# Query-key attention layer: three of four quads of value rows weighed by VectorE, one by POOL, and scans that start from PSUM

## What is computed

```python
q = (x @ Wq + bq).reshape(n, 8, 32); k = ...; v = ...
scores = einsum('ehd,ehd->eh', q[src], k[dst]) / sqrt(32)
m = segment_max(scores, dst)
e = exp(scores - m[dst])
z = segment_sum(e, dst)
p = e / maximum(z[dst], 1e-16)
out = segment_sum(v[src] * p[:, :, None], dst)
```

## Time and profile before

| what | value |
| --- | --- |
| median of three runs | 6924.0 us (6918.83 to 6942.32) |
| the profiled execution | 6916.7 us |
| its span | 6914.9 us |
| mean granted TensorE clock over the span | 0.808 |
| the changed stage in the span | about 3160 to 4556 us |

### The profile page before, as it was taken

One profiled execution on the slowest core, in us unless ns is written; L12 is line 12 of the kernel. 1 busy time (PEld: TensorE's weight loads), 2 busy tenths in 40 slices (PEclk: granted clock), 3 DMA queues, 4 the chain that ended last, 5 costly groups with the idle time before them and its releaser, 6 DMA issues. The chain is left out here.

```text
span 6914.9 us, 124558 instructions
## 1 busy us (share of the span) xinstructions
PE 4848.1 (70%) x21021; PEld 3523.0 (51%) x21022; DVE 5023.9 (73%) x11704; ACT 3845.9 (56%) x9024; POOL 4869.6 (70%) x4954
## 2 busy tenths in 40 slices
PE   6563277777647777775777777769999974777775
PEld 5452155555435555554555555546667653455553
DVE  6665377777757777787888888875555556777777
ACT  2341277677637676753444444426777763666664
POOL 0576677777477777757778878757777765777773
PEclk9655578788868888788989998979999985877777
DMA  5222255555335555525666666624444433555553
GB/s 166 66 70 53 80 135 137 135 137 135 92 92 136 136 135 137 134 77 147 187 178 187 181 187 179 184 72 130 129 130 130 130 102 103 136 135 135 135 134 91
DMA packets 596188, 894.68 MB, mean 129 GB/s; under 512 B 322611, under 2 KB 372960, under 8 KB 595700
## 3 DMA queue, kind: packets, MB, share of 16 engines
q0 software_dynamic: 245984, 649.30, 34.4%
q1 hardware_dynamic: 349700, 218.85, 11.9%
q10 hardware_dynamic: 416, 25.60, 1.1%
HBM read 859.36 MB, written 59.47 MB: 133 GB/s over the span
## 5 line engine op out<-in xcount | busy, mean ns | idle before, releaser
L1501 POOL DMA_INDIRECT at_ring<-tab_s,at_idx x808 | 776.0, 960 | 277.3 <-issue 204.7
L2391 POOL DMA_INDIRECT ae_ring<-tab_a,ae_idx x808 | 772.5, 956 | 256.0 <-issue 228.1
L1501 POOL DMA_INDIRECT at_ring_0a<-tab_s,at_idx_0a x808 | 767.5, 950 | 256.3 <-issue 206.9
L2001 POOL DMA_INDIRECT ad_ring<-tab_qv,ad_idx x808 | 772.9, 957 | 248.7 <-issue 208.0
L1501 POOL DMA_INDIRECT at_ring_0b<-tab_s,at_idx_0b x808 | 767.2, 950 | 255.4 <-issue 210.0
L1677 PE MATMUL at_po<-at_rows,at_hot 128*128 128x260 f32 x1616 | 557.6, 504 | 141.1 <-DVE at_begin L104 83.4
L1677 PE MATMUL at_po_0a<-at_rows_0a,at_hot_0a 128*128 128x264 f32 x1616 | 554.5, 500 | 139.6 <-DVE at_begin_0a L104 80.3
L1677 PE MATMUL at_po_0b<-at_rows_0b,at_hot_0b 128*128 128x264 f32 x1616 | 552.3, 499 | 138.9 <-DVE at_begin_0b L104 93.9
L2206 PE MATMUL ad_pk<-node_a,ad_hr 128*128 x1616 | 457.1, 432 | 223.3 <-DVE ad_prod L2076 122.1
L2285 ACT ACTIVATE ad_hot<-iota_row,ad_nrel 128x128 f32<-128x128 f32 x808 | 256.5, 388 | 462.0 <-PE ad_po L2225 462.0
L1677 PEld LDWEIGHTS at_po<-at_rows,at_hot 128*128 128x128 f32 x1616 | 384.2, 250 | 239.3 <-DVE at_begin L104 112.2
(11 more groups left out here) (521 smaller groups left out, 12537.1 us busy)
## 6 DMA issues: line engine op xcount, KB each, us to landing
at_rr_0a<-relrow_d SPq DMA_DIRECT2D x102, 256.0 KB
at_rr_0b<-relrow_d SPq DMA_DIRECT2D x102, 256.0 KB
ad_rr<-relrow_d SPq DMA_DIRECT2D x102, 256.0 KB
at_rr<-relrow_s SPq DMA_DIRECT2D x102, 256.0 KB
ae_feat<-attr_pad SPq DMA_DIRECT2D x808, 32.0 KB
rnk_lrow<-lorow_f SPq DMA_DIRECT2D x98, 256.0 KB
attr_pad<-in_edge_attr_dram ACTq DMA_DIRECT2D x1, 25000.0 KB, 81.8
at_ring_0a<-tab_s,at_idx_0a POOLq DMA_INDIRECT x808
```

The costliest lines, as they stand in the source:

```text
L1501: eng.indirect_dma_start(out=ring[:, t.slot * STEP + u, :], out_offset=None, in_=table, in_offset=bass.IndirectOffsetOnAxis(ap=idx[:, t.sl ...
L2001: eng.indirect_dma_start(out=ring[:, t.slot * STEP + u, :], out_offset=None, in_=table, in_offset=bass.IndirectOffsetOnAxis(ap=idx[:, t.sl ...
L2391: eng.indirect_dma_start(out=ring[:, k, :], out_offset=None, in_=table, in_offset=bass.IndirectOffsetOnAxis(ap=idx[:, k:k + 1], axis=0))\
```

## The change

VectorE weighs quads 0, 1 and 2 and POOL quad 3 alone. VectorE's new multiply stands between `dot2` and `prod6`; it reads `pe` directly, as `rows0` and `rows1` do. POOL's is still issued after the first quad of gathers. `al` and the copy `weights` shrink to one quad. `begin` and `end` are gone: `full` and `top` take `col2` and `col4` in PSUM as initial values, and `shrink` reads `col2`. TensorE waits for VectorE instead of POOL before the sums of quad 2.

```diff
-             "prod4", "prod5", "dot2", "prod6", "prod7", "dot3", "add4", "fwd", "add5", "add6", "add7",
-             "col1", "carried", "carry", "add8", "add9", "begin", "full", "bwd", "add10", "add11", "col2", "back",
-             "add12", "add13", "end", "top", "under", "shrink", "add14", "add15", "weights", "factor"]
-        B = ["rows2", "rows3"]
+             "prod4", "prod5", "dot2", "rows2", "prod6", "prod7", "dot3", "add4", "fwd", "add5", "add6", "add7",
+             "col1", "carried", "carry", "add8", "add9", "full", "bwd", "add10", "add11", "col2", "back",
+             "add12", "add13", "top", "under", "shrink", "add14", "add15", "weights", "factor"]
+        B = ["rows3"]
...
-            al = sb(f"ad_al_{tag}", [P, H, HALF], F32, c)
+            al = sb(f"ad_al_{tag}", [P, H, QUAD], F32, c)
...
-                        if q == 2:
-                            eng.wait_ge(vec, v.at("weights", t.plus(-1)))
+                        eng.wait_ge(vec, v.at("weights", t.plus(-1)))
...
                     with eng.Fori(0, TURNS // BUF - 1) as i:
                         for k in range(BUF):
-                            weigh_rows(2, turn(i, k + 1))
                             gather(turn(i, k + 2))
-                    weigh_rows(2, last(1))
                     gather(last(2), quads=TAIL)
-                    for q in (2, 3):
-                        weigh_rows(q, last(2))
-                    for q in range(2, TAIL):
-                        weigh_rows(q, last(3))
+                    weigh_rows(3, last(2))
...
                         def weigh_rows(q):
-                            if not sums:
+                            if not sums or q >= quads:
                                 return v.skip(f"rows{q}")
...
                         dot(2)
+                        weigh_rows(2)
                         products(6)
...
-                            v.did("begin", copy(eng, begin[:, :], col2))
-                            done("begin", t)
-                            v.did("full", eng.tensor_tensor_scan(full[:, :], brk, logits, begin[:, 0:1], ALU.add, ALU.max))
+                            v.did("full", eng.tensor_tensor_scan(full[:, :], brk, logits, col2, ALU.add, ALU.max))
...
-                            v.did("end", copy(eng, end[:, :], col4))
-                            done("end", t)
-                            v.did("top", eng.tensor_tensor_scan(top[:, ::-1], brk_after, full[:, ::-1], end[:, 0:1],
+                            v.did("top", eng.tensor_tensor_scan(top[:, ::-1], brk_after, full[:, ::-1], col4,
...
-                            v.did("shrink", eng.tensor_scalar(less[:, P:P + 1], begin[:, :], top[:, 0:1], 0.0,
+                            v.did("shrink", eng.tensor_scalar(less[:, P:P + 1], col2, top[:, 0:1], 0.0,
...
-                                eng, al[:, :, :], pe[:, 0:R].rearrange("p (h u) -> p h u", h=H)[:, :, HALF:STEP]))
+                                eng, al[:, :, :], pe[:, 0:R].rearrange("p (h u) -> p h u", h=H)[:, :, 3 * QUAD:STEP]))
...
-                                    if q < 2:
+                                    if q < 3:
                                         eng.wait_ge(vec, v.at(f"rows{q}", t))
```

More of the change, by code:

```diff
@@ L1874, in attend_dot @@
             top = sb(f"ad_max_{tag}", [R, P], F32, c)
-            begin = sb(f"ad_begin_{tag}", [R, 1], F32, c)
-            end = sb(f"ad_end_{tag}", [R, 1], F32, c)
             line_f = sb(f"ad_linef_{tag}", [1, H, STEP], F32, c)
@@ L1990, in weigh_rows @@
                         g.did(f"rows{q}", eng.tensor_tensor(
-                            to, to, al[:, :, (q - 2) * QUAD:(q - 1) * QUAD].rearrange("p h u -> p u h")
+                            to, to, al[:, :, :].rearrange("p h u -> p u h")
                             .rearrange("p u (h o) -> p u h o", o=1).to_broadcast([P, QUAD, H, CW]), ALU.mult))
@@ L2007, in gather @@
                         moving.send(eng, t.lap, t.slot, range(2))
-                    g.skip("rows2", "rows3")
-                    eng.sem_inc(wtd, 2)
+                    g.skip("rows3")
+                    eng.sem_inc(wtd, 1)
                     g.behind = 0
@@ L2141, in step @@
                         else:
-                            v.skip("begin", "full", "bwd")
+                            v.skip("full", "bwd")
                         add(10, 11)
@@ L2161, in step @@
                             v.did("under", eng.tensor_tensor(less[:, 0:P], logits, top[:, :], ALU.subtract))
-                            v.did("shrink", eng.tensor_scalar(less[:, P:P + 1], begin[:, :], top[:, 0:1], 0.0,
+                            v.did("shrink", eng.tensor_scalar(less[:, P:P + 1], col2, top[:, 0:1], 0.0,
                                                               ALU.subtract, ALU.min))
                         else:
-                            v.skip("end", "top", "under", "shrink")
+                            v.skip("top", "under", "shrink")
                         add(14, 15)
```

## The result

The changed kernel takes 6965.8 us (median of 4 runs, 6962.8 to 6968.0) against 6922.8 us for the kernel before on the same chip (4 runs, 6918.8 to 6942.3). The ratio is 1.0063, 95% interval 1.0051 to 1.0076: slower by 0.6%, inside the range of 6930 to 6973, 15 us above the predicted 6951.

A forecast was written before the change was run, and what follows sets the result against it. The prediction took VectorE's back-to-back path to set the turn, with TensorE's clock deciding its waits for keys. Its terms summed to +0.55 us a turn, 27 us over 49 turns, giving 6951 us, range 6930 to 6973.

The forecast's parts named there:

- The multiply and the gap it fills: VectorE weighing the third quad adds 1.17 us a turn; standing between third reduction and next product saves 0.21.
- PSUM as a scan's initial value: Scans and shrink reading a column of PSUM in place of SBUF: taken as 0 us a turn.
- The far end of the prediction: Scans and shrink: each of three PSUM reads costs 59 ns more, +0.18 us a turn.
- The copies: Begin and end removed from VectorE's path, each ahead of a scan: 0.38 us less a turn.
- POOL owns only the held scan: POOL's multiply delays VectorE only at scan L2124, 503 ns against 411; moving it saves 0.09 us a turn.
- price of 0.237: Estimated microseconds a turn loses for each microsecond TensorE's clock is at its lower level: 0.237.
- Rival (c): POOL is the bound after all; freeing its queue shortens a turn by up to 0.81 us, 6884 us; chance 0.06.
- 27.13 - x: The changed kernel's turn in us if POOL owns x of the 1.26 us a turn put down to the clock.
- Cover: VectorE's new multiply hides its 1.02 us wait for TensorE's last keys in 10 of 48 turns: -0.20 us a turn.
- Clock: TensorE's mean granted clock falls from 0.90 to 0.88 as turn and idle stretch lengthen: +0.30 us a turn.
- TensorE's wait for the fourth reduction: TensorE's standstill between its fourth set of sums and the score transpose grows from 0.75 to about 1.7 us.
- Other stages: Sign of being wrong: stages that are not edited move by more than a few microseconds.

The follow-up runs named there:

- e2: The kernel before with only the copies begin and end removed, POOL still weighing two quads; 6936.4 us, ratio 1.0021 to the kernel before.
- e3: The kernel before with nobody weighing the third quad of value rows, its sums running over unweighed rows; 6899.4 us, ratio 0.9968 to the kernel before.
- e1: The changed kernel with the copies begin and end put back; 6954.4 us, ratio 1.0046 to the kernel before.
- e4: The changed kernel with POOL weighing the fourth quad twice, giving POOL its old load; 6969.5 us, ratio 1.0068 to the kernel before.
- e12: The changed kernel, VectorE's group-number load behind its first multiply, nine empty instructions at its layer part's end; 6958.3 us, ratio 1.0044 to the kernel before.
- e11: The kernel before with 23 empty instructions ending VectorE's query-key layer part; ratio 0.9990 in runs where the kernel before took 9616 us.

## Why the prediction was right, and where it was wrong

The direction was right, and the layer's own number nearly so: +28.6 us against 27, +0.62 us a turn against +0.55. By the steps:

- **The multiply and the gap it fills** (+1.17 - 0.21). Right. In the changed full-clock turn the product behind the new multiply starts at 4180.43, 2.29 us after the third reduction at 4178.14; before it was 1.35. That is +0.94 against +0.96.
- **PSUM as a scan's initial value** (0). Right: 479 ns for L2128 against 480 for L2137, and 208 against 204 ns for the shrink. In the same kernel but for the copies (e2) the two scans take 478 and 482 ns, where the kernel before has 480 and 484. The far end of the prediction, 59 ns more for each of three reads, is not shown for the initial value, and at 4 ns hardly for the shrink.
- **The copies** (-0.38). Right for a full-clock turn (-0.29 and -0.32), wrong for the mean (+0.02 in the changed kernel, -0.02 in the kernel before). I took VectorE's path as the one that sets every turn. In the kernel before it was not: the time went into the held scan (503 to 1023 ns in e2). In the changed one the time at the lower level rose as the copies went (5.5 to 6.0 us a turn).
- **"POOL owns only the held scan"** (-0.09). This is the step that failed. The held scan did go (L2117 at 412 ns), but e3 puts POOL's share at up to 0.84 us. I read 0.09 as what POOL costs, when it was only what was left of the hold in a VectorE slowed by other things; made faster, VectorE is held for up to 0.61 us a turn (1023 - 412 ns in e2). The other 0.75 us of e3 came with less time at the lower level, 5.1 to 2.1 us a turn; at the prediction's own price of 0.237 that is 0.71 us (an estimate). Rival (c) had the mechanism, a VectorE "stopped at L2124 by the multiply", but not the outcome: with 0.84 us owned by POOL its 27.13 - x gives 26.29 us, and the changed kernel takes 27.29. I judged POOL by waits that name it, and there are none. The sum came out right by luck: freed queue -0.84, multiply +1.44 (not +0.96) and copies +0.02 make +0.62, where the forecast reached +0.55 with smaller terms on both sides. Each of these measured steps includes what the clock did. The prediction also counted only nine waits of POOL beyond "issue"; 16 more name L2234 (4.8 us in total, 0.7 at most), and one of 2.0 us names an index load. That changes nothing in the sum.
- **Cover** (-0.20). Hardly earned: the waits for keys went from 43.4 to 41.7 us in the 48 turns, 0.04 us a turn.
- **Clock** (+0.30). Right in sign. The clock stands at 0.89, not 0.88, and the mean turn is 1.84 us longer than the full-clock turn (27.29 - 25.45) against 1.60 before: +0.24. The price of 0.237 us for each microsecond at the lower level was my estimate from the earlier trace rows; the changed kernel's 1.84 us over its 6.0 would make it 0.31. TensorE's wait for the fourth reduction grew about as foretold, to 1.7 us at most and 1.46 in the mean of 44 (before 0.8 at most and 0.66 in the mean of 48). From the waits of the changed kernel in its 48 turns:

```profile
PE ad_tt L2234 <- DVE ad_dots L2076: 64.2, 44, 1.7
```

- **Other stages.** The prediction called it wrong if they moved by more than a few microseconds. They did: +14.6 in the message layer. The profiled executions differ by 48.5 us where 27 were forecast, and this layer is the largest part of the excess, before the last part's 6.5. The edit that removes the copies, not the multiply, brings it (e1, e2), by a mechanism that is not found.

No kernel tried with the right output beats the kernel before. Two edits that this points to were not tried: TensorE's load moved off the head of the turn, and VectorE's third multiply put into the time in which it waits for the first keys.

## What to carry to other kernels

A queue that is packed to the microsecond may be the bound though no wait names it; remove its load once and look at the turn (here 0.84 us shorter in e3), rather than add up the waits, and compare the length of one and the same instruction across kernels: here a scan went from 412 to 1023 ns. Before hiding an engine's idle time, look what the other engines do in the same microseconds: here TensorE was late by as much, and 54 us of hidden idle time bought nothing. Compare the stages that an edit does not touch too, since taking out two 0.15 us copies made a later layer 15 us longer.

## What the runs showed of the hardware that I had not expected

- Work off VectorE did not shorten the mean turn of the changed kernel. With the copies (e1), without them, with a second POOL multiply (e4) and with VectorE's load hidden (e12) it is 27.27 to 27.30 us, while the full-clock turn ranges from 25.43 to 26.13. In the changed kernel most turns fall into a few lengths (25.4, 25.9, 27.5, 28.3) that recur in a fixed order with the changes of the granted clock. The mean turn lies above the full-clock one by 1.84 us in the changed kernel, 1.53 in e1, 1.16 in e4 and 1.87 in e12, which made up for the difference each time; how is open.
- The scan over two SBUF inputs that met a POOL multiply ended 0.28 us after it, 1.37 us long in the kernel before and 2.22 us in e2, and its group takes 412 ns in the mean once the multiply stands elsewhere. Why the scan is held beside the multiply was not shown.
- A load of 16 group numbers into an engine's registers took 1.10 us on TensorE and on VectorE alike, once a turn. The lists of waits name it on neither.
- One chip ran the kernel before in 6923 us in one set of runs and in 9616 in another; in the latter VectorE of e11 was idle for up to 6.7 us at a time. Comparisons hold only within one set.
